# Delta rule of a Perceiver block: one query group convolved by VectorE, the triangle applied between levels, tap products in one run, key-query products behind the levels

## The reference

```python
q = silu(causal_depthwise_conv(h @ Wq, conv_q))     # 4 taps per channel
k = silu(causal_depthwise_conv(h @ Wk, conv_k))
v = silu(causal_depthwise_conv(h @ Wv, conv_v))
gk = -exp(A_log) * softplus(h @ Wgk + dt_bias)
beta = sigmoid(h @ Wb + b_b)
q = l2norm(q) * SCALE ; k = l2norm(k)
def step(S, inp):                                   # over the 128 rows, per head
    S = S * exp(gt)
    kv = einsum('bhk,bhkv->bhv', kt, S)
    delta = (vt - kv) * bt
    S = S + einsum('bhk,bhv->bhkv', kt, delta)
    ot = einsum('bhk,bhkv->bhv', qt, S)
    return S, ot
o = rmsnorm(o) * g_norm_weight * g * sigmoid(g) ; return o @ Wo
```

## Time and profile before

| | us |
|---|---|
| median of three timed runs | 907.89 |
| lowest and highest of them | 906.61 and 909.77 |
| the profiled execution | 913.58 |
| its span, first to last instruction | 911.9 |
| the delta net's block in it | 448.6 to 533.3 |
| its levels, first and last product | 477.2 to 508.7 |

### The profile page before, as it was taken

The page is one execution under the profiler, slowest core; times in us unless marked ns, Lnnn a source line. Parts: engine busy times, 40 slices in busy tenths (PEclk is TensorE's granted clock), DMA queues, the critical chain, the costliest instruction groups (busy, mean ns, idle before and its releaser), DMA issues. The chain is left out here.

```text
span 911.9 us, 22117 instructions
## 1 busy us (share of the span) xinstructions
PE 881.2 (97%) x8498; PEld 563.1 (62%) x8498; DVE 690.5 (76%) x1221; ACT 487.4 (53%) x1158; POOL 299.9 (33%) x443
## 2 busy tenths in 40 slices
PE   9999999999999999999898989999999999999898
PEld 5445554555455455665778867666777766777675
DVE  3499879878987898999465657877888888788426
ACT  2544454355345445444379423556767666666753
POOL 5563365346435633664207425300011000000000
PEclk9999999999999999999999999999999999999999
DMA  9467847564574457432511246686666666667100
GB/s 166 173 189 212 248 186 198 143 202 113 136 188 176 104 144 212 146 101 73 181 50 54 72 127 167 177 250 168 169 170 169 169 169 170 177 190 196 38 3 6
DMA packets 115082, 136.38 MB, mean 150 GB/s; under 512 B 65720, under 2 KB 86992, under 8 KB 114992
## 3 DMA queue, kind: packets, MB, share of 16 engines
q1 hardware_dynamic: 111280, 134.23, 52.8%
q10 hardware_dynamic: 3712, 0.92, 0.7%
HBM read 81.48 MB, written 53.07 MB: 148 GB/s over the span
## 5 line engine op out<-in xcount | busy, mean ns | idle before, releaser
L2094 DVE TENSOR_REDUCE mx<-bank 128x1 f32<-128x896 f32 x224 | 233.6, 1085 | 48.4 <-PE bank L1937 45.1
L2155 ACT ACTIVATE p<-bank 128x512 f32<-128x512 f32 x392 | 202.5, 602 | 96.4 <-PE bank L1981 96.2
L721 DVE STREAM_TRANSPOSE ew<-sc 32x896 f32<-32x896 f32 x208 | 229.4, 1103 | 27.7 <-ACT sc L805 20.2
L580 PE MATMUL bank<-Wv,ctxT 128*128 128x512 f32 (+1 forms) x308 | 133.7, 574 | 0.0
L1994 PE MATMUL bank<-p,v 128*32 128x128 f32 x3136 | 106.8, 277 | 0.9 <-issue 0.9
L1994 PEld LDWEIGHTS bank<-p,v 128*32 128x32 f32 x3136 | 80.3, 110 | 31.3 <-ACT p L2155 27.7
L580 PEld LDWEIGHTS bank<-Wv,ctxT 128*128 128x128 f32 x308 | 58.3, 190 | 65.3 <-issue 58.4
L457 POOL CAST kt<-kf 128x512 bf16<-128x512 f32 (+1 forms) x56 | 31.3, 558 | 201.9 <-ACT kf L777 201.9
L1864 POOL TENSOR_SCALAR neg<-run 128x16 f32<-128x16 f32 x14 | 3.6, 257 | 251.3 <-DVE run L2109 251.3
L1981 PE MATMUL bank<-home,krest 99*128 99x128 bf16 x1008 | 79.6, 220 | 5.7 <-DMA home<-n3T 3.8
L1981 PEld LDWEIGHTS bank<-home,krest 99*128 99x128 bf16 x1008 | 64.3, 98 | 30.1 <-issue 6.6
(11 more groups left out here) (353 smaller groups left out, 1264.1 us busy)
## 6 DMA issues: line engine op xcount, KB each, us to landing
krest<-kscr SPq DMA_DIRECT2D x36, 384.0 KB, 6.3
vscr<-vpair SPq DMA_DIRECT2D x12, 1004.5 KB, 4.1
kscr<-kt SPq DMA_DIRECT2D x14, 768.0 KB, 3.6
krest<-kscr SPq DMA_DIRECT2D x36, 288.0 KB, 9.3
kscr<-kt SPq DMA_DIRECT2D x14, 576.0 KB, 5.1
v<-vscr SPq DMA_DIRECT2D x14, 574.0 KB, 10.8
vpair<-kscr SPq DMA_DIRECT2D x20, 384.0 KB, 6.1
kscr<-kt SPq DMA_DIRECT2D x14, 512.0 KB, 4.5
```

Source lines behind the costliest of these rows:

```text
L580: ins = pe.matmul(bank[kv_bank(op, s)][:, 0:w * D], turned_context(c)[:, i, k * P:(k + 1) * P], Wv01[:, i, 0:w].rearrange("p w o -> p (w o)"),
L721: dve.transpose(pT0[j * SQ:(j + 1) * SQ, :, :, i * SQ:(i + 1) * SQ].rearrange("m t h q -> m h t q"), rows[:, j]).then_inc(S("turn0"), 1)
L2094: dve.tensor_reduce(mx1[:, c % 2, h:h + 1], psum[:, b:b + 2, :].rearrange("p b n -> p (b n)")[:, 0:CH], AX.X, ALU.max).then_inc(S("smread1 ...
L2155: act.activation(p1[:, g % PR, :], bank[ST1[g % 3]][:], ACT.Exp).then_inc(S("exp1"), 1)
```

## The change

- `hidden` and its three matmuls are removed; Ek and Ec are no longer zero outside the triangle. VectorE multiplies Ec by the triangle (`triangle`, three instructions) behind level 2, after AT has been made.
- Group 3 (two blocks of queries) isn't multiplied by ScalarE and summed by GpSimd any more. VectorE convolves it (`queries_conv`, two scalar steps and six steps of multiply and add over 128 x 128) behind level 1.
- ScalarE's tap products come in one run, groups 2, 4, 5, 6, with the silus and the squares of the queries behind them. The slots of `vp` are given by `TAPSLOT`.
- `norms` of the queries moves from level 4 to level 5. KQ of groups 0 and 1 moves behind the values' transposes, which now use banks `ZB[g]`, and KQ of group 2 behind the products of U by vt. `query_rows` comes after `values_rows`.

```diff
--- before.py
+++ after.py
@@ -887,7 +886,9 @@
 
         GROUPS = ((KB, 4), (KB + 4, 2), (0, 4), (4, 2), (2 * KB, 4), (2 * KB + 4, 4), (2 * KB + 8, 4))
         GBANK = (0, 1, 2, 3, 6, 5, 6)
-        PARTS = (0, 0, 2, 3, 5, 7, 9)
+        PARTS = (0, 0, 2, 0, 4, 6, 8)
+        TAPSLOT = {2: 0, 4: 1, 5: 0, 6: 1}
+        TAPORDER = (2, 4, 5, 6)
         DB, ZB, XB, SIDE = (4, 5, 6), (7, 0, 1), (4, 2, 3), (5, 6, 5)
         KP = (0, 0, 3)
         EBANK = (5, 6, 5, 6, 4, 2, 3, 4)
@@ -944,7 +945,7 @@
                 sp.wait_ge(S("vscr_mid"), 16)
                 sp.wait_ge(S("sg"), NG)
                 gather(sp, 0, 1)
-                sp.wait_ge(S("convp"), 5)
+                sp.wait_ge(S("convp"), 4)
                 gather(sp, 0, 0)
 
             @block.vector
@@ -1026,9 +1027,30 @@
                     dve.wait_ge(S("U1"), g + 1)
                     dve.transpose(X[:, hb(g)], U[:, hb(g)]).then_inc(S("X1"), 1)
 
+                def queries_conv():
+                    b0, n = GROUPS[3]
+                    dve.wait_ge(S("qcopy"), 2)
+                    for j in (TAPS - 1,) + tuple(range(TAPS - 1)):
+                        for b in range(b0, b0 + n):
+                            x, w_ = xpad[:, b, j:j + P], convw[:, b, j:j + 1]
+                            if j == TAPS - 1:
+                                ins = dve.tensor_scalar(cv[:, b], x, w_, None, ALU.mult)
+                            else:
+                                ins = dve.scalar_tensor_tensor(out=cv[:, b], in0=x, scalar=w_, in1=cv[:, b],
+                                                               op0=ALU.mult, op1=ALU.add)
+                        if j == TAPS - 2:
+                            ins.then_inc(S("conv"), 1)
+                        else:
+                            ins.then_inc(S("convstep"), 1)
+                            dve.wait_ge(S("convstep"), nth("convstep"))
+
+                def triangle():
+                    for g in range(NG):
+                        dve.tensor_tensor(Ec[:, hb(g)], Ec[:, hb(g)], bc(tri[:], 1, [P, GH, P]), ALU.mult).then_inc(S("DT"), 1)
+
                 def values_rows(g):
                     dve.wait_ge(S("vT"), g + 1)
-                    dve.tensor_tensor(vt[:, hb(g)], b4(SIDE[g]), bc(rk[:, hb(g)], 2, [P, GH, P]), ALU.mult).then_inc(S("vt"), 1)
+                    dve.tensor_tensor(vt[:, hb(g)], b4(ZB[g]), bc(rk[:, hb(g)], 2, [P, GH, P]), ALU.mult).then_inc(S("vt"), 1)
 
                 def query_rows(g):
                     dve.wait_ge(S("KQ"), max(g + 1, 2))
@@ -1041,11 +1063,9 @@
                             dve.transpose(U[:, hb(g)], X[:, hb(g)]).then_inc(S("U"), 1)
                         dve.wait_ge(S("Zmm"), NG * (n - 1) + g + 1)
                         dve.tensor_tensor(Y[:, hb(g)], b4c(ZB[g]), bc(levelc[:, n], 1, [P, GH, HALF]), ALU.mult).then_inc(S("Z"), 1)
-                    if n == 4:
+                    if n == NL:
                         dve.wait_ge(S("n2q"), 1)
                         dve.tensor_scalar(tq[:], bank[SIDE[0]][:, 0:NH], 1e-6, DV * LN_EPS * DK, ALU.add, ALU.mult).then_inc(S("tq"), 1)
-                    if n == NL:
-                        query_rows(2)
                     for g in range(NG):
                         dve.wait_ge(S("XZ"), NG * (n - 1) + g + 1)
                         if n < NL:
@@ -1055,12 +1075,18 @@
                         else:
                             dve.wait_ge(S("U"), NG * (NL - 2) + g + 1)
                             dve.tensor_tensor(U[:, hb(g)], U[:, hb(g)], b4c(XB[g]), ALU.subtract).then_inc(S("U5"), 1)
-                    if n == 4:
-                        query_rows(0)
-                        query_rows(1)
+                    if n == 1:
+                        queries_conv()
+                    if n == 2:
+                        dve.wait_ge(S("AT"), NG)
+                        triangle()
                 dve.wait_ge(S("rk"), 2)
                 for g in range(NG):
                     values_rows(g)
+                dve.wait_ge(S("DT"), NG)
+                query_rows(0)
+                query_rows(1)
+                query_rows(2)
 
                 for g in range(NG):
                     dve.wait_ge(S("dmm"), g + 1)
@@ -1109,15 +1135,15 @@
                     b0, n = GROUPS[g]
                     if part == 0:
                         act.wait_ge(S("cproj"), g + 1)
-                        if g >= 4:
-                            act.wait_ge(S("convp"), g - 3)
+                        if g >= 5:
+                            act.wait_ge(S("convp"), g - 4)
                     for j in range(2 * part, 2 * part + 2):
                         for k in range(TAPS):
                             late, w_ = TAPS - 1 - k, convw[:, b0 + j, k:k + 1]
                             if g < 4:
-                                ins = act.activation(vp[:, k, g % 2, j], xpad[:, b0 + j, k:k + P], ACT.Copy, scale=w_)
+                                ins = act.activation(vp[:, k, TAPSLOT[g], j], xpad[:, b0 + j, k:k + P], ACT.Copy, scale=w_)
                             else:
-                                ins = act.activation(vp[:, k, g % 2, j, late:], bank[GBANK[g]][:, j * P:(j + 1) * P - late],
+                                ins = act.activation(vp[:, k, TAPSLOT[g], j, late:], bank[GBANK[g]][:, j * P:(j + 1) * P - late],
                                                      ACT.Copy, scale=w_)
                     ins.then_inc(S("vp"), 1)
 
@@ -1175,25 +1201,16 @@
                 products(2, 0)
                 gate(2)
                 products(2, 1)
-                products(3, 0)
-                products(4, 0)
-                for n in range(1, NL):
-                    if n == 1:
-                        products(4, 1)
-                        products(5, 0)
-                        products(5, 1)
-                    if n == 2:
-                        silu(2, "convp", 1)
-                        silu(3, "convp", 2)
-                        act.wait_ge(S("silu"), 4)
-                        act.activation(sq[:, KB:2 * KB], cv[:, 0:KB], ACT.Square).then_inc(S("sqq"), 1)
-                        products(6, 0)
-                        products(6, 1)
-                    if n == 3:
-                        silu(4, "convp", 3)
-                        silu(5, "convp", 4)
-                    if n == 4:
-                        silu(6, "convp", 5)
+                for g in TAPORDER[1:]:
+                    products(g, 0)
+                    products(g, 1)
+                silu(2, "convp", 1)
+                silu(3, "conv", 3)
+                act.wait_ge(S("silu"), 4)
+                act.activation(sq[:, KB:2 * KB], cv[:, 0:KB], ACT.Square).then_inc(S("sqq"), 1)
+                silu(4, "convp", 2)
+                silu(5, "convp", 3)
+                silu(6, "convp", 4)
                 for g in range(NG):
                     act.wait_ge(S("wmm"), g + 1)
                     act.copy(w[:, hb(g)], b4(XB[g])).then_inc(S("w"), 1)
@@ -1314,10 +1331,7 @@
                 for g in range(NG):
                     if g == 2:
                         pe.wait_ge(S("v1mid"), CT)
-                    if g == 0:
-                        pe.wait_ge(S("hidden"), 1)
-                    pe.matmul(b4(DB[g]), ident[:], bc(hidden[:], 1, [P, GH, P]), start=True, stop=False)
-                    pe.matmul(bank[DB[g]][:], below[:], R[:, hb(g)].rearrange("p h t -> p (h t)"), start=False,
+                    pe.matmul(bank[DB[g]][:], below[:], R[:, hb(g)].rearrange("p h t -> p (h t)"), start=True,
                               stop=True).then_inc(S("dsum"), 1)
                 pe.wait_ge(S("masks"), MASKS)
                 pe.wait_ge(S("qcopy"), 2)
@@ -1344,13 +1358,10 @@
                         else:
                             pe.wait_ge(S("X"), NG * (n - 2) + g + 1)
                         blocks(g, ZB[g], lambda r, h: AT[r, h, r], lambda r, h: X[r, h], "Zmm", HALF)
-                    if n == 4:
+                    if n == NL:
                         pe.wait_ge(S("sqq"), 1)
                         pe.wait_ge(S("vp"), PARTS[5])
                         norms(SIDE[0], KB, "n2q")
-                    if n == NL:
-                        pe.wait_ge(S("at"), 2)
-                        against_keys(2, SIDE[0], 0, "KQ")
                     for g in range(NG):
                         pe.wait_ge(S("Z"), NG * (n - 1) + g + 1)
                         if n > 1:
@@ -1365,22 +1376,19 @@
                     if n == 2:
                         pe.wait_ge(S("vp"), PARTS[4])
                         project(6)
-                    if n == 4:
-                        pe.wait_ge(S("tq"), 1)
-                        pe.wait_ge(S("vp"), PARTS[6])
-                        against_keys(0, SIDE[0], 0, "KQ")
-                        against_keys(1, SIDE[0], 0, "KQ")
                 for g in range(NG):
-                    if g < 2:
-                        pe.wait_ge(S("at"), 3)
-                    else:
-                        pe.wait_ge(S("vt"), 1)
```

(16 more changed lines are left out.)

1 line of the change is left out of this document (removed).

## The result

The changed kernel takes 912.7 us in the median of 20 executions, the kernel before 910.0 in as many: ratio 1.0033, 95% interval 1.0019 to 1.0047, so it is slower by 3.0 us, 1.7 to 4.3. The prediction had +1.2 us against its base of 907.9, most likely a difference too small to tell. The time itself lies inside its range (902.0 to 913.0), but the difference is 1.8 us more than forecast, clear of zero, and just beyond the 2.7 us (0.3%) that the prediction took as the least it could tell.

The account below looks back on a forecast made before the run. TensorE, busy for 97% of the span, was taken as the bound. Gains of 6.2 us against 6.3 for the VectorE train and 1.1 for the clock gave +1.2 us: 909.1 from a median of 907.9, range 902.0 to 913.0.

Parts of the forecast that it names:

- Part 1: Decay sums: three `hidden` matmuls leave TensorE's queue, `norms` starts near 468.16 instead of 470.74; gain 2.5 us.
- Part 2: Before `project(6)`: reordered ScalarE tap products end TensorE's wait of 2.29 us and the low clock's 1.55; gain 3.8 us.
- Part 5: VectorE's eight convolution steps take turns with GpSimd's passes at SBUF: 8.7 us instead of 2.4, 6.3 more; chance 0.38.
- pushed back: Rival: each VectorE step also delays GpSimd's next pass; train of 12.7 us, +5.7, 913.6 us; chance 0.15.
- Whole train: Rival: VectorE's eight steps keep the ports after one wait; -4.3, 903.6 us; chance 0.17.
- no collision: Rival: VectorE's steps and GpSimd's sums don't collide for these operands; 901.7 us; chance 0.13.
- two at a time: Rival: a tap's two VectorE steps fit behind each GpSimd pass; train of 6.8 us, 907.9 us; chance 0.15.
- The clock behind it: After TensorE's pause at level 2 the clock falls again, slowing the second product and projection: 1.1 us, 0 to 1.6.
- Part 3: Behind the levels: `norms` and key-query products moved, the 0.48 us gap at the values' transposes goes; gain 0.5, 0 to 0.8.
- Part 4: VectorE's added work without collision: eight steps of 2.4 us overrun its idle time by 0.6; triangle hidden behind `project(6)`, costing nothing.
- if GpSimd left VectorE alone: Sum for the whole change without collision between the two engines: 2.5 + 3.8 + 0.5 - 0.6 = 6.2 us faster.

Follow-up runs that it names:

- e10_before_look: The unchanged kernel before, profiled a second time: block 83.6 us, `project(6)` 2.05 us, granted clock 1.00 behind the pause.
- e4_part1: The kernel before without the `hidden` matmuls, triangle multiplied by VectorE behind level 2, nothing else changed: ratio to before 0.9972, block 82.0 us.
- e12_before_look2: The unchanged kernel before, profiled a third time: block 83.6 us, `project(6)` 2.05 us after a pause of 2.28.
- e8_halves: The changed kernel with each GpSimd pass of 128x512 made as two of 128x256: ratio to before 0.9995, block 82.5 us.
- e1_yield: The changed kernel with GpSimd's sums of groups 4, 5 and 6 held until VectorE's convolution is through: ratio to before 1.0007, block 84.1 us.
- e3_spin: The changed kernel with 23 dummy matmuls in TensorE's long pause of level 2: ratio to before 1.0028, block 84.3 us.
- e11_spin_again: The changed kernel with 23 dummy matmuls in level 2's pause, run a second time: ratio to before 1.0021, block 84.3 us.
- e7_gaps_old3: Changed kernel, convolution and triangle moved to VectorE's gaps, but `norms`, key-query products and values' transposes back in their old places: ratio to before 0.9979, block 83.3 us.
- e2_early: The changed kernel with VectorE's eight convolution steps moved earlier, half behind `sq`, half behind `ck`: ratio to before 0.9965, block 80.0 us.
- e9_before_spin: The kernel before with nine dummy matmuls in TensorE's pause before `project(6)`: ratio to before 1.0010, block 83.6 us.
- e6_gaps: The changed kernel with the convolution early and the triangle moved into VectorE's gaps of levels 1 and 2: ratio to before 0.9928, block 77.8 us.

## Why the prediction was right or wrong

**Part 1** (-2.5 us): right in its mechanism, 0.4 too large. `norms` starts at 468.15, just behind the squares (467.13 + 0.96) as forecast, against 470.41 in e10_before_look, with nearly the same start of the block (448.30 and 448.27): 2.3, of which 2.1 are left when level 2 begins (484.46 and 486.59). e4_part1 has 2.2 there, and was timed at -2.5.

**Part 2** (-3.8): half right. The pause that ScalarE's products ended is gone (-2.3). The other 1.55 was the low clock behind it, and this is the step that failed first: I took what one execution of before showed for something that every one pays. Two further profiles with the same pause don't have it (2.05 for `project(6)`), and filling the pause showed no gain. In the block it makes 1.1 us (1.55 less the gap of 0.46 that opens without it). Since its share among the timed executions is open, so is how much of the 1.55 the medians lack. The profiled execution was 5.7 us above the median of the timed runs, which should have made me take a second profile; by itself it said nothing of this place, for e12_before_look2 is longer still (915.3 us) and has no fall there.

**Part 5, the train** (8.7 us instead of 2.4): right, and in its mechanism the best part of the prediction. It was 8.6, and 8.5 in the second profile; TensorE's pause "over 6" was 6.14 and 6.10. (The sum had 0.6 + 6.3 = 6.9 for it, 0.8 too much by its own words.) Each step stands behind one GpSimd pass (1.37 against my 1.31), and all but one of the passes stay at 1.27 us, so "pushed back" fell. "Whole train" and "no collision" fell with the length of the train, "two at a time" with e8_halves. The rule of the Trainium skill (SBUF — State Buffer, "Who interferes with whom"), by which a VectorE instruction with two SBUF inputs or in a two-port mode shuts GpSimd's reads out for its whole length and the other way round, is borne out by this trace in one direction: beside passes of 1.27 us the steps take 1.37, alone 0.35. In the other direction the short steps cost GpSimd nothing that the rows show (its passes start 1.34 apart beside the train and 1.35 apart alone, in e1_yield), while the longer multiplications of the triangle do hold it up. e8_halves shows besides that the turns go by single instructions, so the short ones pay for the long ones. The scalar steps of the first tap, where I had allowed "no collision", can collide too: one took 281 ns, the other 1296.

**The clock behind it** (1.1, 0 to 1.6): the second term of the wrong size. The second product of level 2 and `project(6)` took 2.83 and 3.15; with the clock kept in e3_spin they take 2.00 and 2.05, so the low clock cost 1.9 us. I had argued that VectorE paces the first of them anyway, which it does at 2.00, not at 2.83; and the slow stretch reached through most of `project(6)` as well. The second profile has 2.83 and 2.81: 1.6. The timed runs of e3_spin and e11_spin_again don't confirm the size.

**Part 3** (-0.5, 0 to 0.8): a little too small: -1.3. Against e10_before_look, level 3 starts 4.0 us later (494.07 and 498.05) and the block ends 2.7 later (531.88 and 534.58). Three gaps of TensorE account for it: the 0.48 that I had counted, the 0.46 before the key-query products, closed in the profile that I read, and 0.35 of a wait for R behind the output (0.67 to 0.32). That it is worth more where the rest is in time, e7_gaps_old3 shows.

**Part 4, the triangle** (nothing): right for this kernel, in part by luck. It is hidden under `project(6)` (495.42 to 497.31, within 494.97 to 498.12), as forecast. But it takes only 1.89 us because the late train puts it behind GpSimd's sums; in e1_yield and e2_early it meets them, takes 2.3 to 3.0 us longer, and TensorE waits. So the 6.2 us "if GpSimd left VectorE alone" were not to be had by placing the convolution alone.

**The sum.** Against an execution of before without the low clock:

| | us |
|---|---|
| forecast | +1.2 |
| low clock of before not there | +1.6 |
| part 1 at 2.1 for 2.5 | +0.4 |
| low clock of the changed kernel at 1.9 for 1.1 | +0.8 |
| VectorE's pace in the product behind the pause (2.00 for 1.76) | +0.2 |
| pause at 6.1 for 6.9 | -0.8 |
| part 3 at 1.3 for 0.5 | -0.8 |
| together | +2.6 |

The blocks show 2.7, and 2.3 in the second profile; the timed runs show 3.0 and 2.5. So the failed step is the low clock, on both sides: counted as a sure gain of 1.55 where before need not have it, and at 1.1 where the changed kernel pays 1.9. From the rows alone, at the start of level 3: -2.1 (part 1, as level 2 begins) + 6.14 - 2.29 (the pauses) + 2.2 (the two slow rows) = +4.0, and 4.0 is what the two traces show.

**Open.** Why the 2 us that the dummy matmuls save in the block appear in the timed runs as 0.5 to 1, and e9_before_spin, unchanged in the block, as +0.9: the intervals cover both. In how many executions of before the clock falls behind the pause of 2.29 us, and so whether its median lacks all of the 1.55 or a part.

## What to carry to other kernels

Before work with two SBUF inputs goes to VectorE, look at what GpSimd does in that very stretch, not only whether VectorE is idle: a train of short steps beside long GpSimd instructions costs one GpSimd instruction for each step, while the same eight steps some 15 us earlier (468.1 for 482.9) cost nothing. When a collision is moved, follow GpSimd's work to where it now lands, since it may meet the next VectorE step of that kind. And before a low clock in one trace is put into a sum, take a second profile of the same kernel: here two of three lacked it. With one profile alone, such a term belongs in the range and not in the sum.

## What the runs showed of the hardware that I had not expected

*The same pause, either clock.* Four executions have the pause of 2.28 or 2.29 us before `project(6)`: in two the clock then was low (before, e4_part1), in two it stayed (e10_before_look, e12_before_look2). Pauses of 1.73 (e2_early) and 2.00 (e1_yield) left it alone, one of 1.93 in e7_gaps_old3 did not; the pauses of 2.43 (e1_yield), 2.75 (e8_halves) and 6.1 (the changed kernel, twice) were all followed by it. In before it is 1.00 through the whole pause and 0.50 from 493 on; in the changed kernel it falls within the pause (0.62 from 490 to 492). The rows don't tell what decides.

*Long VectorE instructions do hold GpSimd up.* The 128x128 steps left its passes at 1.27 us (one at 1.33 to 1.36 in each profile), the 128x512 multiplications of the triangle lengthened them to 1.59 to 1.72 (e1_yield) and were themselves lengthened from 0.68 to 1.50 to 1.75 each. GpSimd's power function of 128x12, 2.29 us long, didn't hold up the two multiplications of e6_gaps that ran beside it (0.67 and 0.68).

*Where single executions differ.* Behind the block, with the same code in all kernels, the profiles took from 374.8 us (e3_spin) to 382.7 (e9_before_spin). One place of it, in two profiles of before (the first row is of e10_before_look, with a span of 908.4 us, the second of e12_before_look2, with 913.6):

```profile
600.25 0.54 PE L1937 MATMUL bank<-krest,home 96*128 96x512 bf16 x2
...
600.38 1.01 PE L1981 MATMUL bank<-home,krest 99*128 99x128 bf16 x8 [3.23 <-DMA home<-n3T]
```

The second waited 3.23 us for a DMA, and then its clock was low (0.53 from 600 to 605, against 1.00). Such waits come and go between executions of the same program and are as large as the whole effect studied here, so the spans of one profile of each kernel can't tell a difference of 3 us. The block's own length can, if it is known whether a low clock is in it: before's blocks of 84.7 and 83.6 us differ by that alone.
